# Late edge groups gather normalised source rows from DRAM

## The chip, the cores and the metric

One core of a Trainium2 chip. The metric is the device time of one launch in microseconds, lower is better. Engines are named as in the profile: PE (matmul, with PEld its weight loads), DVE (vector), ACT (scalar, activations), POOL (GpSimd) and SP (sync, which issues plain DMAs).

## The reference

One message-passing layer over N = 50000 nodes and E = 25000 edges, rows of H = 128 float32, edges sorted by target:

```
h        = max(layernorm(x), 0)
em       = relu(layernorm([h[src], h[dst]] @ msg_w + msg_b) * g + beta) * edge_weight
messages = segment_sum(em, dst) / counts          (0 where a node has no edge)
gate     = sigmoid(h @ gate_w + gate_b)
h_new    = relu(layernorm([h, messages] @ upd_w + upd_b) * g + beta)
out      = x + gate * h_new + (1 - gate) * h
```

`layernorm` of x has no gain or shift, so `h` of a node depends on its row of x alone. Both ends of an edge need `h`, not x; the last line needs x of the target.

## The kernel before

**Two stages, in groups of 512 rows.** A group is 128 partitions times G = 4 rows. The node stage runs NG = 98 groups over all nodes as if none had an edge (message zero) and stores the result to `out`. The edge stage runs EG = 49 groups of 512 edges, sums the messages along the sorted edges, computes the update for each edge's target, and scatters the rows of targets with edges over `out` (where an edge is not its target's last, the index is out of bounds and nothing is written). So scatters must come behind the node stores.

**Software pipeline.** Each engine runs the same list of steps; in step s it works on group s, s-1, ... at different stages. Node: x loaded by SP (`node_step`, L505), statistics in DVE step s (L715), `nb` = -mean * rstd (`minus_mean`, L385) and `h` = relu(x * rstd + nb) on ACT in step s+1 (`node_h`, L1093, into `hrow`, 4 buffers), transposed by PE (`flip`, L1200), multiplied, then `mix` (L452: out = x + (1-gate) * h, on DVE in step s+4, into `o`, 4 buffers) and `final` in step s+6. SP stores `o` of group s-8 in step s, and `xload` has XS = 8 buffers. The last six node steps run together with edge steps 0 to 5.

Edge: for group g, source rows and target rows of x have been gathered into a slot of `ring` (RING = 32 slots, each with a source and a target half). DVE step g takes the statistics of both (L917 and L938), with `moment` (L362) in place of an aggregate. ACT step g+1 computes `h` of the source rows into `hrow` (L1145), then of the target rows into `h_dst` (L1151); PE step g+1 flips both (L1276, L1297); then the message product (step g+2), its scaling (`gamma_m`, step g+3), the running sum (step g+4), the update (step g+5), `mix` (step g+7, into `o[g % 4]`) and `final` (step g+8). At the end of the edge stage, from step 49, steps only drain and get shorter.

**POOL** issues all gathers and scatters, one indirect DMA for each 128 rows, in an order written out by hand:

1. The source rows of groups 0 to 4 (EARLY = 5).
2. Beside the node stage, spread over its 98 groups and paced by each group's `mix` (L631 to L644): all other source and target rows of groups 0 to 31, and target rows of groups 35 to 48 (STAGED = 14), which SP stores to DRAM and reloads by plain DMA in the edge stage.
3. Source rows of groups 32 to 38 (AHEAD = 7), as soon as `h` of the group 32 back has been computed (L647).
4. A wait for all node stores, then for each edge group g: wait for `final` of g and for the flips of g+6, four scatters (L667), and a share of the refills (L668): the list is spread over groups 0 to 35 (REFILLED = 36) and holds the source rows of groups 39 to 48 and the target rows of groups 32 to 34.

`mix` of group g waits until the scatter of group g-4 has landed, since both use `o[g % 4]`:

```python
                if fin and not drained:
                    ed["rest"].after(dve, g)
                    if beyond(g, 4):
                        dve.wait_ge(s_scat[g.at % 4], g.rounds(16 * G))
```

Everything behind that on DVE (sums, mix, moments of the newest group) waits with it. In the draining steps (from 49) the same wait stands at the step's start (L906).

**SP** in the edge stage stores the running sums of each group and reloads staged target rows; its last waits are for all stores and scatters.

Of the kernel before, what the change touches and what calls it, by code (L numbers as in the profile page):

```python
# [42 lines left out]
G = 4  # L43
# [4 lines left out]
EG = J // G  # L48
# [6 lines left out]
AHEAD = 7  # L55
# [95 lines left out]
def build(nc, x, src, dst, edge_weight, msg_w, msg_b, msg_g, msg_beta, upd_w, upd_b, upd_g, upd_beta,  # L151
# [3 lines left out]
    with ctx:  # L155
# [12 lines left out]
        staged_dram = nc.dram_tensor("staged_target_rows", (STAGED * P, G * H), f32).ap()  # L168

# [123 lines left out]
        s_st = sem4("node_rows_stored")  # L293
        s_gsrc = sem4("source_rows_gathered")
# [66 lines left out]

        def moment(L, g, n, which):  # L362

            s4 = (g.at + 1) % 4
            v = st[:, g.at % 4, 0:n, :]
            if which == 0:
                nc.vector.tensor_tensor(mv[:, s4, 0:n, 0], v[:, :, 1], v[:, :, 4], ALU.add)
                nc.vector.tensor_tensor(s_dif[:, 0:n], v[:, :, 1], v[:, :, 4], ALU.subtract)
                L.mark(nc.vector.tensor_tensor(s_var[:, 0:n], v[:, :, 2], v[:, :, 5], ALU.add))
            elif which == 1:  # L370
                L.mark(nc.vector.tensor_tensor(s_dif[:, 0:n], s_dif[:, 0:n], s_dif[:, 0:n], ALU.mult))
            else:
                L.mark(nc.vector.scalar_tensor_tensor(mv[:, s4, 0:n, 1], s_dif[:, 0:n], H / 4, s_var[:, 0:n],
                                                      ALU.mult, ALU.add))

        def logs(act, d, s, k, scale=1.0):
            one_mark(d["ln"], act, s, nc.scalar.activation(lnv[:, s.at % 4, 0:k], mv[:, s.at % 4, 0:k, 1], ACT.Ln,  # L377
                                                           bias=eps_col[:, :], scale=scale))

        def rstds(act, d, s, k):  # L380
            act.wait_ge(d["ln"].sem, s.times(1, 1))
            one_mark(d["rstd"], act, s, nc.scalar.activation(rs[:, s.at % 4, 0:k], lnv[:, s.at % 4, 0:k], ACT.Exp,
                                                             scale=-0.5))

        def minus_mean(dve, d, g, n, factor=-1.0):  # L385
            d["rstd"].after(dve, g.back(-1))
            s4 = (g.at + 1) % 4
            one_mark(d["nb"], dve, g, nc.vector.scalar_tensor_tensor(  # L388
                nb[:, s4, 0:n], mv[:, s4, 0:n, 0], factor, rs[:, s4, 0:n], ALU.mult, ALU.mult))
# [96 lines left out]
        def _(sp):  # L486
# [68 lines left out]
            for i in range(4):  # L555
                sp.wait_ge(s_st[i], 16 * len(range(i, NG, 4)))
                sp.wait_ge(s_sums[i], 16 * len(range(i, EG, 4)))
                sp.wait_ge(s_scat[i], 16 * G * len(range(i, EG, 4)))
# [5 lines left out]
        def _(pool):  # L564
# [36 lines left out]
            def gather(dest, rows, idx, s):  # L601
                pool.indirect_dma_start(out=dest, out_offset=None, in_=rows,  # L602
                                        in_offset=bass.IndirectOffsetOnAxis(ap=idx, axis=0),
                                        **(if_tail if rows is x else {})).then_inc(s, 16)
# [19 lines left out]
            for g in range(EARLY):  # L624
                for k in range(G):
# [3 lines left out]
                        for part in ((gather_dst,) if g < EARLY else (gather_src, gather_dst)) for k in range(G)]  # L629
# [28 lines left out]
            for g in range(EG):  # L658
# [10 lines left out]
                for part, q, k in refills[refilled:upto]:  # L669
                    if k == 0 and part is gather_src:  # L670
                        ed["h"].after(pool, Group(q - RING), 1)
                    elif k == 0:
                        ed["mix"].after(pool, Group(q - RING))
                    assert q - RING <= g + (AHEAD if part is gather_src else 0)
                    part(q, k)
# [9 lines left out]
        def _(dve):  # L685
# [203 lines left out]
            def edge_step(s, node=None):  # L889
# [24 lines left out]
                if new:  # L914
                    dve.wait_ge(s_gsrc[s.at % 4], s.rounds(G * 16, G * 16))
                    L = ed["stats"]
                    row_stats(L, s, slot(s, 0), 0)  # L917
                if live(s.back(1), EG):
                    minus_mean(dve, ed, s.back(1), 2 * G, -0.5)
# [133 lines left out]
        def _(act):  # L1053
# [49 lines left out]
            def edge_step(s, node=None):  # L1103
# [6 lines left out]
                logs(act, ed, s, 4 * G, 1.0 / H)  # L1110
                rstds(act, ed, s, 4 * G)
# [29 lines left out]
                if live(g, EG):  # L1141
# [3 lines left out]
                    H_.mark(h_rows(g, hrow[:, (g.at + NG) % 4], slot(g, 0), 0))  # L1145
# [4 lines left out]
                if live(g, EG):  # L1150
                    H_.mark(h_rows(g, h_dst[:, (g.at + NG) % XS], slot(g, 1), G))  # L1151
# [47 lines left out]
        def _(pe):  # L1199
# [53 lines left out]
            def edge_step(s):  # L1253
# [92 lines left out]
```

## Time and profile before

| | |
|---|---|
| median of 3 runs | 909.52 us (909.29 to 910.0) |
| profiled execution: time | 908.32 us |
| profiled execution: span, first to last instruction | 906.6 us |
| mean granted clock of TensorE | 0.924 |
| DMA, whole span | 107.96 MB |

The profiler records one execution. Busy time doesn't count register, branch, semaphore and DMA-issuing instructions of SP; a GpSimd indirect DMA is shown as the time that POOL spends on it, not that of its data. The engine's next instruction can start before the one shown has ended, so two starts are a better measure of what an instruction costs than its duration. "L602" is a line of the kernel; L602 is the helper `gather`, L607 `scatter`, L353 `row_stats`, L395 `h_rows`, L454 `mix_row`, L480 `final`, L388 `minus_mean`, L894 the `omg` instruction at the start of a DVE edge step. `ring<-in_x,src_i` is a gather of source rows, `ring<-in_x,gidx` one of target rows, `work<-in_x,gidx` one of target rows that will be staged, `out<-work,sidx` a scatter.

### The profile page before, as it was taken

Reading aid. Unit: us, or ns where it says so; the run is one execution under the profiler, and the core shown is the slowest. Engines: PE = TensorE matmul, PEld = TensorE weight load, DVE = VectorE, ACT = ScalarE, POOL = GpSimd, SP = SyncE. Lnnn points to the kernel's source line nnn. Section 1 sums busy time; section 2 is a strip of 40 time slices with the busy share of each in tenths; the row PEclk is TensorE's granted clock in tenths of the full one; section 3 lists DMA queues with packets and bytes.
Section 4 is the critical chain, followed back from the end, with each engine's and each line's share of the span. In section 5 each row is a group of like instructions: output and inputs, shape, how many; then the busy total and the mean of one; then the engine's idle time right before and its main releaser. Section 6 shows DMA issues by size and latency. Waiting matters only on the chain.

```text
span 906.6 us, 20426 instructions
## 1 busy us (share of the span) xinstructions
PE 664.2 (73%) x4448; PEld 530.6 (59%) x4448; DVE 847.5 (93%) x3820; ACT 834.8 (92%) x3476; POOL 608.9 (67%) x602
## 2 busy tenths in 40 slices
PE   1877777877777777768578778777787787877871
PEld 0555555655555556555466667666676676666760
DVE  6799999999999999999998999999999999999994
ACT  2799999999999999999789999999999999999972
POOL 4777776666666666666557777657776666664467
PEclk9999999899999999999869998999989999899885
DMA  5355555556556566555223232332211211211111
GB/s 152 97 177 168 175 166 172 162 174 194 177 179 185 182 179 187 176 184 162 73 68 101 66 105 84 103 100 81 83 63 62 70 58 64 71 52 55 58 63 34
DMA packets 60436, 107.96 MB, mean 119 GB/s; under 512 B 14566, under 2 KB 16438, under 8 KB 60370
## 3 DMA queue, kind: packets, MB, share of 16 engines
q1 hardware_dynamic: 39756, 71.88, 23.7%
q0 software_dynamic: 18912, 34.84, 14.4%
q10 hardware_dynamic: 1702, 0.53, 0.3%
q8 instruction: 21, 0.34, 0.2%
q14 instruction: 45, 0.37, 0.1%
HBM read 56.01 MB, written 55.12 MB: 123 GB/s over the span
## 4 chain that ended last, share of the span: by engine, by line
ACT 44%; DVE 36%; issue 10%; PE 4%; POOL 3%; DVEq 1%; ACTq 1%; DMA 1%; POOLq 0%
ACT junk L402 11%; DVE work L752 9%; DVE work L454 9%; ACT hrow L395 9%; ACT xload L395 7%; DVE st L353 6%; ACT work L433 6%; POOL out L607 3%; DVE mv L359 3%; ACT at L1069 2%; ACT work L1126 2%; ACT work L1124 2%; DVE work L731 2%; ACT lnv L377 2%; DVE e L444 2%
## 5 line engine op out<-in xcount | busy, mean ns | idle before, releaser
L607 POOL DMA_INDIRECT out<-work,sidx x196 | 201.7, 1029 | 121.9 <-issue 57.6
L602 POOL DMA_INDIRECT ring<-in_x,src_i x196 | 205.0, 1046 | 79.0 <-issue 54.6
L602 POOL DMA_INDIRECT ring<-in_x,gidx x140 | 142.1, 1015 | 51.0 <-issue 39.0
L395 ACT ACTIVATE hrow<-xload,nb,rs 128x128 f32<-128x128 f32 x392 | 164.4, 530 | 1.6 <-DVE nb L388 1.6
L402 ACT ACTIVATE junk<-py 128x128 bf16<-128x128 f32 x588 | 155.2, 296 | 1.0 <-PE py L1289 1.0
L402 ACT ACTIVATION_READ_ACCUMULATOR junk<-py 128x1 f32 x588 | 133.6, 230 | 0.0
L1203 PE MATMUL pa<-ident,work 128*128 128x128 f32 x376 | 62.6, 290 | 92.6 <-DVE work L731 92.4
L1245 PE MATMUL py<-w_u,work 128*128 128x129 f32 x784 | 119.6, 298 | 0.0
L1245 PEld LDWEIGHTS py<-w_u,work 128*128 128x128 f32 x784 | 99.9, 200 | 21.8 <-issue 21.8
L1203 PE MATMUL pt<-ident,hrow 128*128 128x128 f32 x588 | 101.6, 301 | 13.1 <-ACT hrow L395 12.9
L454 DVE SCALAR_TENSOR_TENSOR work<-hrow,omg,xload 128x128 f32<-128x128 f32 x392 | 108.5, 338 | 0.0
L1203 PEld LDWEIGHTS pa<-ident,work 128*128 128x128 f32 x376 | 40.6, 144 | 115.6 <-issue 112.1
L752 DVE SCALAR_TENSOR_TENSOR work<-pm,gt,work 128x128 f32<-128x128 f32 x376 | 105.1, 341 | 0.0
L1268 PE MATMUL pm<-w_all,work 128*128 128x128 f32 x392 | 98.3, 340 | 0.0
L353 DVE BATCH_NORM_STATS2 st<-xload 128x6 f32<-128x128 f32 x392 | 98.0, 278 | 0.1
L1270 PE MATMUL pm<-w_all,work 128*128 128x128 f32 x392 | 93.6, 329 | 0.0
L1203 PEld LDWEIGHTS pt<-ident,hrow 128*128 128x128 f32 x588 | 76.4, 156 | 21.6 <-ACT hrow L395 20.7
L353 DVE BATCH_NORM_STATS2 st<-ring 128x6 f32<-128x128 f32 x392 | 84.8, 278 | 0.2
L602 POOL DMA_INDIRECT work<-in_x,gidx x56 | 55.6, 994 | 42.3 <-DVE work L454 42.3
L1287 PE MATMUL py<-w_all,at 128*128 128x128 f32 x392 | 82.6, 293 | 0.0
L1268 PEld LDWEIGHTS pm<-w_all,work 128*128 128x128 f32 x392 | 74.8, 237 | 12.7 <-issue 12.7
L395 ACT ACTIVATE hrow<-ring,nb,rs 128x128 f32<-128x128 f32 x196 | 82.3, 532 | 0.0
(170 smaller groups left out, 1832.6 us busy)
## 6 DMA issues: line engine op xcount, KB each, us to landing
xload<-in_x SPq DMA_DIRECT2D x98, 256.0 KB
out<-work SPq DMA_DIRECT2D x98, 256.0 KB
running_sums<-acc SPq DMA_DIRECT2D x49, 256.0 KB, 2.1
staged_target_rows<-work SPq DMA_DIRECT2D x14, 256.0 KB, 3.6
ring<-staged_target_rows SPq DMA_DIRECT2D x14, 256.0 KB, 3.1
ring<-in_x,src_i POOLq DMA_INDIRECT x196, 3.0
out<-work,sidx POOLq DMA_INDIRECT x196, 2.2
ring<-in_x,gidx POOLq DMA_INDIRECT x140
```

What stands on the lines that cost most here:

```text
L353: last = nc.vector.bn_stats(st[:, g.at % 4, at + m, :], rows[:, m, :])
L395: last = nc.scalar.activation(dest[:, m, :], rows[:, m, :], ACT.Relu, bias=nb[:, s4, at + m:at + m + 1], scale=rs[:, s4, at + m:at + m + 1])
L402: last = nc.scalar.activation(junk[:, j, k, :], prod[:, k, 0:H], ACT.Square, scale=scale, accum_out=mv[:, slot, at + k, 1:2])
L454: return nc.vector.scalar_tensor_tensor(dest[:, k, :], h[:, k, :], omg[:, g.at % 4, k:k + 1], xr[:, k, :], ALU.mult, ALU.add)
L602: pool.indirect_dma_start(out=dest, out_offset=None, in_=rows, in_offset=bass.IndirectOffsetOnAxis(ap=idx, axis=0), **(if_tail if rows is ...
L607: pool.indirect_dma_start(out=out, out_offset=bass.IndirectOffsetOnAxis(ap=idx, axis=0), in_=rows, in_offset=None, **if_tail).then_inc(s, 16)
L752: last = nc.vector.scalar_tensor_tensor(o[:, f.at % 4, k, :], pm[:, k, :], gt[:, f.at % 4, k:k + 1], o[:, f.at % 4, k, :], ALU.mult, ALU.add)
L1203: last = nc.tensor.transpose(dest[:, k * H:(k + 1) * H], rows[:, k, :], ident[:, :])
L1245: last = nc.tensor.matmul(py[:, g.at % 2, k, 0:H + 1], ht_dst[:, g.at % 4, k * H:(k + 1) * H], w_u1[:, :], start=False, stop=k % 2 == 1)
L1268: nc.tensor.matmul(pm[:, k, :], ht_src[:, g.at % 2, k * H:(k + 1) * H], w_all[:, 0, :], start=False, stop=False)
L1270: last = nc.tensor.matmul(pm[:, k, :], ht_dst[:, (g.at + NG) % 4, k * H:(k + 1) * H], w_all[:, 1, :], start=False, stop=k == G - 1)
L1287: nc.tensor.matmul(py[:, g.at % 2, k, 0:H], at_[:, g.at % 2, k * H:(k + 1) * H], w_all[:, 3, :], start=False, stop=False)
```

## The change

- The node stage stores `hrow` of every group (256 KB each, 25.7 MB in all) to a new DRAM tensor `normalised_rows`. SP issues the store of group s-4 in step s, behind the store of `out` of group s-8. ACT waits for it before it overwrites the buffer.
- Edge groups from LATE = 16 gather their source rows from there. For these groups DVE takes no statistics of the source half, `moment`, `minus_mean`, the logarithm and the reciprocal root work on a narrower range, ACT computes no `h` of source rows, and PE transposes the gathered rows straight from the ring. The target half is as before; ACT's two marks for `h` now stand behind its first two and last two rows.
- POOL's order: beside the node stage, source rows of groups 5 to 15 alone and target rows of 0 to 31. Then a wait for all stores of normalised rows, the source rows of groups 16 to 27 (UPFRONT = 12) in one go, then scatters and refills as before, the refills now being source rows of groups 28 to 48 and target rows of 32 to 34 over the same 36 groups.
- SP's small bias load moves from behind the first eight node loads to ahead of the load of node group 4.

```diff
-AHEAD = 7
+LATE = 16
+UPFRONT = 12
+        h_dram = nc.dram_tensor("normalised_rows", (N, H), f32).ap()
...
     (SP, node_step)
+                q = s.back(4)
+                if live(q, NG):
+                    nd["h"].after(sp, q)
+                    if q.turn is None and q.at == NG - 1:
+                        sp.wait_ge(s_hst[(q.at - 1) % 4], q.back(1).rounds(16, 16))
+                    sp.dma_start(rows(h_dram, q), hrow[:, q.at % 4]).then_inc(s_hst[q.at % 4], 16)
...
             for g in range(1, XS):
+                if g == 4:
+                    sp.wait_ge(s_bsplit, 1)
+                    sp.dma_start(bias3[:, :], bias_b[0:1, :, :]).then_inc(s_b3, 16)
                 node_step(Group(g))
-            sp.wait_ge(s_bsplit, 1)
-            sp.dma_start(bias3[:, :], bias_b[0:1, :, :]).then_inc(s_b3, 16)
...
     (POOL)
-                gather(slot(Group(g), 0)[:, k, :], x, src_i[:, c:c + 1], s_gsrc[g % 4])
+                gather(slot(Group(g), 0)[:, k, :], h_dram if g >= LATE else x, src_i[:, c:c + 1], s_gsrc[g % 4])
...
-                        for part in ((gather_dst,) if g < EARLY else (gather_src, gather_dst)) for k in range(G)]
+                        for part in ((gather_src, gather_dst) if EARLY <= g < LATE else (gather_dst,)) for k in range(G)]
...
-            for g in range(AHEAD):
-                ed["h"].after(pool, Group(g), 1)
+            for i in range(4):
+                pool.wait_ge(s_hst[i], 16 * len(range(i, NG, 4)))
+            for g in range(LATE, LATE + UPFRONT):
                 for k in range(G):
-                    gather_src(g + RING, k)
-            refills = [(part, g, k) for g in range(RING, EG)
-                       for part in (((gather_src,) if g >= RING + AHEAD else ()) + ((gather_dst,) if g < DIRECT else ()))
+                    gather_src(g, k)
+            refills = [(part, g, k) for g in range(LATE + UPFRONT, EG)
+                       for part in ((gather_src,) + ((gather_dst,) if RING <= g < DIRECT else ()))
                        for k in range(G)]
...
     (DVE, edge_step)
                 if new:
-                    dve.wait_ge(s_gsrc[s.at % 4], s.rounds(G * 16, G * 16))
                     L = ed["stats"]
-                    row_stats(L, s, slot(s, 0), 0)
+                    if not late(s):
+                        dve.wait_ge(s_gsrc[s.at % 4], s.rounds(G * 16, G * 16))
+                        row_stats(L, s, slot(s, 0), 0)
...
     (ACT, node_h)
                     nd["nb"].after(act, g)
+                    if beyond(g, 4):
+                        act.wait_ge(s_hst[g.at % 4], g.rounds(16))
...
     (ACT, edge_step)
-                    H_.mark(h_rows(g, hrow[:, (g.at + NG) % 4], slot(g, 0), 0))
+                    if late(g):
+                        H_.mark(h_rows(g, h_dst[:, (g.at + NG) % XS, 0:2], slot(g, 1)[:, 0:2], G))
+                    else:
+                        if g.at < 4:
+                            act.wait_ge(s_hst[(g.at + NG) % 4], 16 * len(range((g.at + NG) % 4, NG, 4)))
+                        H_.mark(h_rows(g, hrow[:, (g.at + NG) % 4], slot(g, 0), 0))
...
-                    H_.mark(h_rows(g, h_dst[:, (g.at + NG) % XS], slot(g, 1), G))
+                    a = 2 if late(g) else 0
+                    H_.mark(h_rows(g, h_dst[:, (g.at + NG) % XS, a:G], slot(g, 1)[:, a:G], G + a))
...
     (PE, edge_step)
-                    ed["h"].after(pe, g, 1)
-                    one_mark(ed["flip"], pe, g, flip(pt[:, 0, :], hrow[:, (g.at + NG) % 4]))
+                    if late(g):
+                        pe.wait_ge(s_gsrc[g.at % 4], g.rounds(G * 16, G * 16))
+                        one_mark(ed["flip"], pe, g, flip(pt[:, 0, :], slot(g, 0)))
+                    else:
+                        ed["h"].after(pe, g, 1)
+                        one_mark(ed["flip"], pe, g, flip(pt[:, 0, :], hrow[:, (g.at + NG) % 4]))
```

## Rows read from the trace of the kernel before

**Rows 1.** Profile page: its head, and busy time by engine

```profile
span 906.6 us, 20426 instructions
...
PE 664.2 (73%) x4448; PEld 530.6 (59%) x4448; DVE 847.5 (93%) x3820; ACT 834.8 (92%) x3476; POOL 608.9 (67%) x602
```

**Rows 2.** Windows, 300 to 400 us (length, busy by engine, clock, DMA share)

```profile
300.00:400.00 100.00, 73.65 (x511) 55.01 (x512) 96.14 (x489) 96.31 (x397) 69.37 (x70) 0.98 0.61 183
```

**Rows 3.** Timeline of DVE in the edge stage (start us, duration us, instruction)

```profile
503.74 0.35 DVE L454 SCALAR_TENSOR_TENSOR work<-xload,omg,ring 128x128 f32<-128x128 f32 x1
...
505.98 0.27 DVE L894 TENSOR_SCALAR omg<-gt 128x4 f32<-128x4 f32 x1
...
506.84 0.86 DVE L353 BATCH_NORM_STATS2 st<-ring 128x6 f32<-128x128 f32 x4
507.85 0.17 DVE L388 SCALAR_TENSOR_TENSOR nb<-mv,rs 128x8 f32<-128x8 f32 x1
...
510.74 0.87 DVE L353 BATCH_NORM_STATS2 st<-ring 128x6 f32<-128x128 f32 x4
511.52 0.68 DVE L942 SCALAR_TENSOR_TENSOR acc<-acc,cont_wb 128x512 f32<-128x512 f32 x1
...
514.62 0.27 DVE L894 TENSOR_SCALAR omg<-gt 128x4 f32<-128x4 f32 x1
...
832.14 0.35 DVE L454 SCALAR_TENSOR_TENSOR work<-xload,omg,ring 128x128 f32<-128x128 f32 x1
```

**Rows 4.** Timeline of POOL from the end of the node stage

```profile
463.54 1.20 POOL L602 DMA_INDIRECT ring<-in_x,src_i  x1 [3.98 <-DVE work L454]
...
477.80 1.99 POOL L602 DMA_INDIRECT ring<-in_x,src_i  x1 [0.30 <-issue]
...
503.37 1.09 POOL L607 DMA_INDIRECT out<-work,sidx  x1 [0.30 <-issue]
504.76 1.50 POOL L607 DMA_INDIRECT out<-work,sidx  x1 [0.31 <-issue]
506.57 1.21 POOL L607 DMA_INDIRECT out<-work,sidx  x1 [0.30 <-issue]
...
509.37 1.05 POOL L602 DMA_INDIRECT ring<-in_x,gidx  x1 [0.30 <-issue]
```

**Rows 5.** Windows of POOL (columns: length, busy, clock, DMA share, GB/s)

```profile
503.37:550.26 46.89, 37.13 (x33) 0.89 0.26 86
550.26:850.00 299.74, 188.77 (x183) 0.91 0.22 72
881.14:904.80 23.66, 18.48 (x18) 0.59 0.11 36
```

**Rows 6.** Chain of waits, inside one edge step

```profile
605.34 1.52 ACT hrow L395 x4
```

**Rows 7.** Groups of POOL's instructions by line, from 463.5 us

```profile
L602 POOL DMA_INDIRECT ring<-in_x,src_i x68 | 76.3, 1122 | 24.4 <-issue 19.2 <-DVE work L454 4.0 <-ACT xload L395 0.9
L602 POOL DMA_INDIRECT ring<-in_x,gidx x12 | 13.3, 1108 | 3.7 <-issue 3.0 <-PE pt L1203 0.3 <-DVE work L454 0.3
```

**Rows 8.** The same groups, 0 to 463.5 us

```profile
L602 POOL DMA_INDIRECT work<-in_x,gidx x56 | 55.6, 994 | 42.3 <-DVE work L454 42.3
```

**Rows 9.** SP's stores near the stage's end; DMA issues with us to landing

```profile
448.88 17.33 SPq L516 DMA_DIRECT2D out<-work  x3
...
running_sums<-acc SPq DMA_DIRECT2D x49, 256.0 KB, 2.1
...
out<-work,sidx POOLq DMA_INDIRECT x196, 2.2
```

**Rows 10.** Timeline of the drain: DVE's last edge group, POOL's last issue

```profile
891.64 0.69 DVE L480 TENSOR_TENSOR work<-work 128x512 f32<-128x512 f32 x1 [0.43 <-ACT work L433]
...
903.82 0.98 POOL L607 DMA_INDIRECT out<-ring,tidx  x1 [0.30 <-issue]
```

**Rows 11.** DMA queues: packets, MB, share of the 16 engines

```profile
q1 hardware_dynamic: 39756, 71.88, 23.7%
```

More of the change, by code:

```diff
@@ L293, in build @@
         s_st = sem4("node_rows_stored")
+        s_hst = sem4("normalised_rows_stored")
         s_gsrc = sem4("source_rows_gathered")
@@ L360, in aggregate, with late @@
             L.mark(last)
+        def late(g):
+            return g.at >= LATE
         def moment(L, g, n, which):
-            s4 = (g.at + 1) % 4
-            v = st[:, g.at % 4, 0:n, :]
+            s4, a = (g.at + 1) % 4, G if late(g) else 0
+            v = st[:, g.at % 4, a:n, :]
             if which == 0:
-                nc.vector.tensor_tensor(mv[:, s4, 0:n, 0], v[:, :, 1], v[:, :, 4], ALU.add)
-                nc.vector.tensor_tensor(s_dif[:, 0:n], v[:, :, 1], v[:, :, 4], ALU.subtract)
-                L.mark(nc.vector.tensor_tensor(s_var[:, 0:n], v[:, :, 2], v[:, :, 5], ALU.add))
+                nc.vector.tensor_tensor(mv[:, s4, a:n, 0], v[:, :, 1], v[:, :, 4], ALU.add)
+                nc.vector.tensor_tensor(s_dif[:, a:n], v[:, :, 1], v[:, :, 4], ALU.subtract)
+                L.mark(nc.vector.tensor_tensor(s_var[:, a:n], v[:, :, 2], v[:, :, 5], ALU.add))
@@ L370, in moment, with logs @@
             elif which == 1:
-                L.mark(nc.vector.tensor_tensor(s_dif[:, 0:n], s_dif[:, 0:n], s_dif[:, 0:n], ALU.mult))
+                L.mark(nc.vector.tensor_tensor(s_dif[:, a:n], s_dif[:, a:n], s_dif[:, a:n], ALU.mult))
             else:
-                L.mark(nc.vector.scalar_tensor_tensor(mv[:, s4, 0:n, 1], s_dif[:, 0:n], H / 4, s_var[:, 0:n],
+                L.mark(nc.vector.scalar_tensor_tensor(mv[:, s4, a:n, 1], s_dif[:, a:n], H / 4, s_var[:, a:n],
                                                       ALU.mult, ALU.add))
-        def logs(act, d, s, k, scale=1.0):
-            one_mark(d["ln"], act, s, nc.scalar.activation(lnv[:, s.at % 4, 0:k], mv[:, s.at % 4, 0:k, 1], ACT.Ln,
+        def logs(act, d, s, k, scale=1.0, a=0):
+            one_mark(d["ln"], act, s, nc.scalar.activation(lnv[:, s.at % 4, a:k], mv[:, s.at % 4, a:k, 1], ACT.Ln,
@@ L378, in logs, with rstds, minus_mean @@
                                                            bias=eps_col[:, :], scale=scale))
-        def rstds(act, d, s, k):
+        def rstds(act, d, s, k, a=0):
             act.wait_ge(d["ln"].sem, s.times(1, 1))
-            one_mark(d["rstd"], act, s, nc.scalar.activation(rs[:, s.at % 4, 0:k], lnv[:, s.at % 4, 0:k], ACT.Exp,
+            one_mark(d["rstd"], act, s, nc.scalar.activation(rs[:, s.at % 4, a:k], lnv[:, s.at % 4, a:k], ACT.Exp,
                                                              scale=-0.5))
-        def minus_mean(dve, d, g, n, factor=-1.0):
+        def minus_mean(dve, d, g, n, factor=-1.0, a=0):
@@ L388, in minus_mean @@
             one_mark(d["nb"], dve, g, nc.vector.scalar_tensor_tensor(
-                nb[:, s4, 0:n], mv[:, s4, 0:n, 0], factor, rs[:, s4, 0:n], ALU.mult, ALU.mult))
+                nb[:, s4, a:n], mv[:, s4, a:n, 0], factor, rs[:, s4, a:n], ALU.mult, ALU.mult))
         def h_rows(g, dest, rows, at):
@@ L556, in _ @@
                 sp.wait_ge(s_st[i], 16 * len(range(i, NG, 4)))
+                sp.wait_ge(s_hst[i], 16 * len(range(i, NG, 4)))
                 sp.wait_ge(s_sums[i], 16 * len(range(i, EG, 4)))
@@ L603, in gather @@
                                         in_offset=bass.IndirectOffsetOnAxis(ap=idx, axis=0),
-                                        **(if_tail if rows is x else {})).then_inc(s, 16)
+                                        **({} if rows is sums_dram else if_tail)).then_inc(s, 16)
             def scatter(rows, idx, s):
@@ L669, in _ @@
                 for part, q, k in refills[refilled:upto]:
-                    if k == 0 and part is gather_src:
-                        ed["h"].after(pool, Group(q - RING), 1)
-                    elif k == 0:
+                    if k == 0 and q >= RING and part is gather_src:
+                        ed["flip"].after(pool, Group(q - RING), 1)
+                    elif k == 0 and q >= RING:
                         ed["mix"].after(pool, Group(q - RING))
-                    assert q - RING <= g + (AHEAD if part is gather_src else 0)
+                    assert q - RING <= g + (5 if part is gather_src else 0)
                     part(q, k)
@@ L914, in edge_step @@
                 if new:
-                    dve.wait_ge(s_gsrc[s.at % 4], s.rounds(G * 16, G * 16))
                     L = ed["stats"]
-                    row_stats(L, s, slot(s, 0), 0)
+                    if not late(s):
+                        dve.wait_ge(s_gsrc[s.at % 4], s.rounds(G * 16, G * 16))
+                        row_stats(L, s, slot(s, 0), 0)
                 if live(s.back(1), EG):
-                    minus_mean(dve, ed, s.back(1), 2 * G, -0.5)
+                    minus_mean(dve, ed, s.back(1), 2 * G, -0.5, G if late(s.back(1)) else 0)
                 q = s.back(3)
@@ L1109, in edge_step @@
                     ed["square_m"].after(act, s.back(3))
-                logs(act, ed, s, 4 * G, 1.0 / H)
-                rstds(act, ed, s, 4 * G)
+                a = G if late(s.back(1)) else 0
+                logs(act, ed, s, 4 * G, 1.0 / H, a)
+                rstds(act, ed, s, 4 * G, a)
                 if node is not None and live(node.back(4), NG):
```

## The prediction

> **What bounds the kernel now.** I read the page's totals first, then the stretches, then one step of the edge stage engine by engine, and last the GpSimd queue, because the change moves work onto it. The totals [rows 1] show DVE and ACT busy for over nine tenths of the span and POOL for two thirds. That average hides two stages. In the node stage DVE and ACT are both at 96 of 100 us and the 16 DMA engines at 0.61 [rows 2]. In the edge stage the step repeats exactly: the `omg` instruction that opens a step on DVE starts at 505.98 and at 514.62 [rows 3], so a step takes 8.64 us, and DVE and ACT are both full in it. POOL comes third, with four scatters and one or two refill gathers a step.
>
> How full POOL is decides this case. Each indirect DMA holds POOL for about 1 us and the next starts 0.30 us later [rows 4], so unstretched issues come 1.28 to 1.35 us apart (0.98 and 1.05 with the gap, rows 4, 10). Once a step one is stretched to about 1.5 and the next to about 1.2: the one that starts at 504.76 ends at 506.26, over the `omg` of 505.98. From 463.54 to 503.37 POOL issued 28 gathers without a real gap, 1.42 us each; then 33 issues in 46.89 us [rows 5], again 1.42. Only later does it wait for anything: between 550 and 850 it is busy 189 of 300 us with 183 issues, and with 0.30 of gap for each some 56 us are truly idle.
>
> **The change, part by part.** (1) *What groups 16 to 48 save.* On DVE the four statistics of the source rows go, 0.78 us (a block of four starts at 510.74, the instruction behind it at 511.52, rows 3); the moment instructions only narrow. On ACT four `h` activations go, 1.52 us [rows 6]. ACT then has slack and DVE sets the step: 8.64 - 0.78 = 7.86, or 7.63 if the wait of 0.23 ahead of `nb` goes too (from 506.84 to 507.85 is 1.01 where the block needs 0.78). Over 33 groups that is 26 to 33 us, if nothing else holds the step.
>
> (2) *What moves to POOL in the edge stage.* Before, source and target gathers of groups 0 to 31 are issued beside the node stage, and 68 + 12 gathers fall behind 463.5 [rows 7]. After, the sources of groups 16 to 31 must wait for the node rows, so there are 48 gathers up front and 84 + 12 = 96 refills: 144 instead of 80. The 64 moved ones were cheap where they stood, since POOL waited there for the node steps' `mix` [rows 8]; taking them away from there saves nothing, as DVE and ACT are the full ones.
>
> (3) *When the gathers up front start.* POOL leaves the node loop behind the `mix` of node group 97, as before, so at 463.54 [rows 4]. The new wait for the stores of normalised rows costs 0 there: SP issues the last of them at about the time of the node stores that begin at 448.88, and a 256 KB store lands in 2 to 4 us (2.1 for the running sums) [rows 9]. The cover is 10 us; without it, POOL would start later by the landing.
>
> (4) *The sum on POOL.* 28 gathers end at 503.37, as now. Twenty more at 1.42: 531.8. Before, scatter(0), the four row scatters of edge group 0, started at 503.37; now at 531.8. It needs 5.3 us to issue and 2.2 to land [rows 9]: 539. DVE's `mix` of group 4 waits for it, as `o` has four buffers; it would have run at 503.74 (group 1, rows 3) + 3 x 8.64 = 529.7. So DVE stalls 9 us there, and behind it in its queue the moments, the sums and, through them, ACT and PE. From there POOL is the bound: a group costs four scatters and 96/36 = 2.67 gathers, 6.67 x 1.42 = 9.5 us, more than the 8.64 of an early step and the 7.7 to 7.9 of a late one, and every DVE step waits at mix(g+4) for scatter(g). 36 groups and the tail's gather: 241 x 1.42 = 342, to 874. Groups 36 to 48 have 52 scatters, with the tail 54 issues. In the last stretch that is free of waits today 18 issues take 23.66 us [rows 5], 1.31 each, fewer of them stretched; I take 1.33: 72 us, to 946. The end lies 1.8 us behind the last issue (906.6 less 903.82 and 0.98, rows 1, 10): span 947.8.
>
> (5) *Is DVE out of the way at the end?* mix(39) ran at 832.14 [rows 3]; now it waits for scatter(35), landed at about 872.7, 40.6 later. From there to final(48), which ended at 892.3 [rows 10], three late steps save 2.4: 930 to 933. POOL reaches scatter(48) at about 939.5, so it stays the bound, by 7 us.
>
> (6) *The node stage.* Each step stores another 256 KB, and SP gets one more wait and one more DMA a step. The SP queue moved 71.88 MB in 23.7% of the 16 engines' span [rows 11], 334 GB/s. 25.7 MB more are 77 us over some 420: +0.18 on the 0.61, less 0.04 for the 64 gathers, about 0.75. ACT's new wait is for the store of group g-4. That is issued behind `final` of g-8, about three steps of 4.6 us ahead, against 2 to 4 us of landing. The loads of x now also queue behind `h` of five groups back, and are still over two steps ahead. I take 0, between -3 (fewer GpSimd issues beside DVE) and +10. The bias load, moved ahead of the load of node group 4, costs 0: three node steps on DVE cover the later loads.
>
> **Sum.** The profiled execution had 906.6 of span in 908.32, so 947.8 gives 949.5. The median of the runs is 1.2 above that execution, inside my error; I say 949. The disputed size is the stretch of the issues. At no stretch 197 scatters take 1.29 and 146 gathers 1.33: 463.5 + 254 + 194 = 912, a time of 915 to 916, still slower than now. Half the stretch gives 932. I take all of it, because the 61 issues in a row had the same DVE instructions beside them.
>
> The trace shows the stretched issues over the step's `omg` and `final` [rows 3, 4]. SBUF — State Buffer in the Trainium skill (SBUF: two separate sides) says that GpSimd can't write descriptors while DVE runs a two-port fast-mode instruction, and gives a DMA that grows from about 620 to 3100 ns. At that price, an estimate from the page, 48 steps with 1.8 us more than I take would come to about 1035; rows 4 show 0.5 and 0.2 us, and the measurement decides.
>
> **The rivals.** *A, POOL keeps pace (faster):* the saving of (1) stands, 908.3 less 26 to 33: 875 to 882. For it: 56 us truly idle on POOL between 550 and 850. Against: 64 x 1.42 = 91 us are added. It decides at 7.8 / 6.67 = 1.17 us an issue, and rows 4, 10 have none under 1.28. Chance 0.06, with other ways to be faster.
> *B, bound by POOL but little stretched:* the DVE step now follows a landing, and its fast instructions may fall where POOL is between issues: 915 to 932. Chance 0.22.
> *C, the stores are paid in the node stage:* if bursts at a share of 0.75 land over a step late, each per cent of 420 us is 4.2; paid in full they are the 77 us of (6), up to 1026; likelier 955 to 975. Against: over two steps of cover. Chance 0.05. The same page of the Trainium skill (A bandwidth-pool intuition that's wrong) says that HBM is almost always the end-to-end bottleneck; the share in rows 2 doesn't bear it out here.
> *D, a longer lock:* every step stretches an issue as the worst one, 1.99 at 477.80 [rows 4], 1.0 over instead of 0.7: 48 x 0.3 = 14 more, 963. It is the skill's lock taken at the worst row. Chance 0.03.
> *E, no measurable change:* saving and deficit cancel, 906 to 912: needs less than no stretch. Chance 0.02.
> *Forecast:* bound by POOL at about 1.4 us an issue, 932 to 960: 0.62.
>
> **How the numbers follow.** What a measurement of this kernel can tell from no change is about 0.2%, 1.8 us. Slower is 0.62 + 0.22 + 0.05 + 0.03 = 0.92, no change 0.02, faster 0.06. The range 920 to 962 holds the forecast and most of B, and leaves out A, E and nearly all of C and D.
>
> **What would show it.** Right: behind 463.5 POOL without waits to the end, 48 gathers first, the first scatter near 532; a period on DVE of 9.4 to 9.6 us for groups 4 to 39 with idle ahead of L454, put down to scatters; ACT far from full in the edge stage; the node stage ending within 3 us of before. Wrong: POOL waiting for `final` in mid-stage, a late period of 7.7 to 7.9 (A); issues of 1.3 us on average in a row (B); DVE waiting for x, or ACT for stores, in the node stage (C).

## The result, and the profile after

| | before | after |
|---|---|---|
| median | 909.76 us (4 runs: 909.29 to 911.79) | 941.93 us (4 runs: 941.4 to 942.47) |
| ratio | | 1.0349 (95%: 1.0331 to 1.0367) |
| span of the profiled execution | 906.6 | 939.7 |

The changed kernel is 32 us slower, 3.5%. The forecast was 949, with a range of 920 to 962.

The page of the changed kernel: its head, busy time by engine, the shares of the chain that ended last, and SP's DMA queue (they answer to [rows 1, 11]).

```profile
span 939.7 us, 20532 instructions
...
PE 684.6 (73%) x4448; PEld 545.7 (58%) x4448; DVE 817.3 (87%) x3688; ACT 786.2 (84%) x3344; POOL 620.3 (66%) x602
...
q1 hardware_dynamic: 53868, 97.58, 29.4%
...
POOL 35%; DVE 34%; issue 18%; PE 6%; ACT 4%; DVEq 1%; DMA 0%; POOLq 0%; ACTq 0%; SPq 0%
```

DVE and ACT each lost 30 to 49 us of busy time and the span grew by 33. In the chain POOL leads with 35%, where the kernel before had ACT with 44% and POOL with 3%:

```profile
ACT 44%; DVE 36%; issue 10%; PE 4%; POOL 3%; DVEq 1%; ACTq 1%; DMA 1%; POOLq 0%
```

Windows of all engines in the changed kernel (length, busy time of PE, PEld, DVE, ACT, POOL, then clock, DMA share and GB/s; the first answers to [rows 2]).

```profile
300.00:400.00 100.00, 77.25 (x510) 57.64 (x508) 95.89 (x485) 95.20 (x394) 53.73 (x54) 0.95 0.73 232
550.00:850.00 300.00, 231.93 (x1519) 195.39 (x1517) 246.34 (x990) 232.18 (x1044) 234.12 (x217) 0.87 0.25 79
```

The second of these stretches in the kernel before, all engines:

```profile
550.00:850.00 300.00, 237.24 (x1635) 201.85 (x1634) 292.67 (x1182) 294.61 (x1249) 189.03 (x184) 0.91 0.22 72
```

The node stage is as it was (95.9 and 95.2 of 100 us), with the DMA share at 0.73 instead of 0.61. In the edge stage DVE has fallen from 98% to 82% and ACT from 98% to 77%. POOL's 234 us with 217 issues leave 66 us, which is the gap of 0.30 behind each one: POOL never waits.

POOL's groups from 463.5 us on [rows 7], L624 being the scatter and L619 the gather:

```profile
L624 POOL DMA_INDIRECT out<-work,sidx x196 | 210.0, 1071 | 59.8 <-issue 58.6 <-PE pt L1231 0.9 <-DVE work L489 0.3
L619 POOL DMA_INDIRECT ring<-normalised_rows,src_i x132 | 144.7, 1096 | 43.9 <-issue 39.9 <-DVE work L463 4.0
L619 POOL DMA_INDIRECT ring<-in_x,gidx x12 | 12.3, 1029 | 3.7 <-issue 3.7
```

POOL's timeline, around the points of the sum [rows 4]:

```profile
463.62 1.20 POOL L619 DMA_INDIRECT ring<-normalised_rows,src_i  x1 [3.99 <-DVE work L463]
...
504.84 1.52 POOL L619 DMA_INDIRECT ring<-normalised_rows,src_i  x1 [0.30 <-issue]
506.66 1.23 POOL L619 DMA_INDIRECT ring<-normalised_rows,src_i  x1 [0.30 <-issue]
...
530.76 0.99 POOL L619 DMA_INDIRECT ring<-normalised_rows,src_i  x1 [0.30 <-issue]
532.05 1.02 POOL L624 DMA_INDIRECT out<-work,sidx  x1 [0.30 <-issue]
...
864.38 1.14 POOL L619 DMA_INDIRECT ring<-normalised_rows,src_i  x1 [0.30 <-issue]
865.83 1.02 POOL L624 DMA_INDIRECT out<-work,sidx  x1 [0.31 <-issue]
...
936.98 0.98 POOL L624 DMA_INDIRECT out<-ring,tidx  x1 [0.30 <-issue]
```

The 48 gathers start at 463.62 and end with the one at 530.76; the first scatter starts at 532.05. The last refill gather is the one at 864.38; from 865.83 on there are only the last 54 issues. None of the 342 issues behind the first starts more than 0.32 us after the end of the one before it.

One late step on DVE, with the wait that now sets it:

```profile
702.75 0.68 DVE L961 SCALAR_TENSOR_TENSOR acc<-acc,cont_wb 128x512 f32<-128x512 f32 x1
706.88 0.35 DVE L981 SCALAR_TENSOR_TENSOR acc<-acc,cont_wb 128x128 f32<-128x128 f32 x1 [3.45 <-issue]
...
709.40 0.29 DVE L912 TENSOR_SCALAR omg<-gt 128x4 f32<-128x4 f32 x1
709.47 0.68 DVE L489 TENSOR_TENSOR work<-work 128x512 f32<-128x512 f32 x1
710.10 0.16 DVE L397 SCALAR_TENSOR_TENSOR nb<-mv,rs 128x4 f32<-128x4 f32 x1
```

Behind L961 DVE stands still for 3.45 us. The next instruction is L981, the running sum, which in program order comes behind `wait_ge(s_scat...)`; the profile calls it "issue" since no DMA landing is matched to it. Over the whole run these waits add up, and ACT's follow from them (us in total, times, longest):

```profile
ACT lnv L386 <- DVE mv L382: 75.2, 36, 7.8
...
DVE acc L981 <- issue: 67.2, 33, 8.7
```

### The profile page after: what moved, and what is told of

Read it like the earlier page. It is cut to its first block, busy times and chain, and to the rows that moved or that the text cites. A ratio compares the mean times of both kernels' runs of the same rounds, so it can differ in the third digit from the quotient of the medians.

```text
span 939.7 us, 20532 instructions
## 1 busy us (share of the span) xinstructions
PE 684.6 (73%) x4448; PEld 545.7 (58%) x4448; DVE 817.3 (87%) x3688; ACT 786.2 (84%) x3344; POOL 620.3 (66%) x602
## 4 chain that ended last, share of the span: by engine, by line
POOL 35%; DVE 34%; issue 18%; PE 6%; ACT 4%; DVEq 1%; DMA 0%; POOLq 0%; ACTq 0%; SPq 0%
POOL out L624 20%; POOL ring L619 16%; DVE work L770 8%; DVE work L463 8%; DVE st L358 6%; DVE mv L364 3%; DVE work L749 2%; ACT hrow L404 2%; PE py L1273 2%; DVE e L453 2%; ACT junk L411 1%; PE pt L1231 1%; DVEq L114 1%; DVE omg L459 1%; PE pa L1231 1%
## 5 line engine op out<-in xcount | busy, mean ns | idle before, releaser
L624 POOL DMA_INDIRECT out<-work,sidx x196 | 210.0, 1071 | 59.8 <-issue 58.6
L619 POOL DMA_INDIRECT ring<-in_x,gidx x140 | 141.0, 1007 | 79.5 <-DVE work L463 43.5
L619 POOL DMA_INDIRECT ring<-normalised_rows,src_i x132 | 144.7, 1096 | 43.9 <-issue 39.9
L981 DVE SCALAR_TENSOR_TENSOR acc<-acc,cont_wb 128x128 f32<-128x128 f32 x196 | 68.0, 347 | 67.5 <-issue 67.2
L1273 PE MATMUL py<-w_u,work 128*128 128x129 f32 x784 | 121.8, 302 | 0.0
L386 ACT ACTIVATE lnv<-mv,eps_col 128x8 f32<-128x8 f32 (+2 forms) x158 | 50.6, 320 | 82.0 <-DVE mv L382 75.2
L619 POOL DMA_INDIRECT work<-in_x,gidx x56 | 55.7, 995 | 91.0 <-DVE work L463 88.9
L463 DVE SCALAR_TENSOR_TENSOR work<-hrow,omg,xload 128x128 f32<-128x128 f32 x392 | 108.5, 339 | 0.0
L1296 PE MATMUL pm<-w_all,work 128*128 128x128 f32 x392 | 103.2, 355 | 0.0
L1298 PE MATMUL pm<-w_all,work 128*128 128x128 f32 x392 | 98.3, 343 | 0.0
L619 POOL DMA_INDIRECT ring<-in_x,src_i x64 | 64.4, 1006 | 41.8 <-DVE work L463 17.0
L1296 PEld LDWEIGHTS pm<-w_all,work 128*128 128x128 f32 x392 | 79.4, 251 | 14.0 <-issue 14.0
L1231 PE MATMUL pt<-ident,hrow 128*128 128x128 f32 x456 | 79.5, 302 | 8.0 <-ACT hrow L404 7.8
L404 ACT ACTIVATE xload<-ring,nb,rs 128x128 f32<-128x128 f32 x196 | 85.1, 525 | 0.0
```

The source lines that it names most:

```text
L404: last = nc.scalar.activation(dest[:, m, :], rows[:, m, :], ACT.Relu, bias=nb[:, s4, at + m:at + m + 1], scale=rs[:, s4, at + m:at + m + 1])
L463: return nc.vector.scalar_tensor_tensor(dest[:, k, :], h[:, k, :], omg[:, g.at % 4, k:k + 1], xr[:, k, :], ALU.mult, ALU.add)
L624: pool.indirect_dma_start(out=out, out_offset=bass.IndirectOffsetOnAxis(ap=idx, axis=0), in_=rows, in_offset=None, **if_tail).then_inc(s, 16)
L981: S.mark(nc.vector.scalar_tensor_tensor(acc[:, m.at % 4, k, :], before, cont_wb[:, m.at * 2 * G + k:m.at * 2 * G + k + 1], acc[:, m.at % 4 ...
L1231: last = nc.tensor.transpose(dest[:, k * H:(k + 1) * H], rows[:, k, :], ident[:, :])
L1273: last = nc.tensor.matmul(py[:, g.at % 2, k, 0:H + 1], ht_dst[:, g.at % 4, k * H:(k + 1) * H], w_u1[:, :], start=False, stop=k % 2 == 1)
```

## The experiments

All are compared with the kernel before run beside them. In experiments 1 to 6 it took 910 us. Six runs came to two other chips, on which the kernel before took 1022 and 1024 us; they stand in a table of their own at the end of this section.

**1. The order of the DMAs alone.**

```diff
         def late(g):
-            return g.at >= LATE
+            return False
...
-                gather(slot(Group(g), 0)[:, k, :], h_dram if g >= LATE else x, src_i[:, c:c + 1], s_gsrc[g % 4])
+                gather(slot(Group(g), 0)[:, k, :], x, src_i[:, c:c + 1], s_gsrc[g % 4])
```

> The changed kernel's DMAs in its order (stores of normalised rows, 48 gathers up front behind them, 96 refills), but every group computes h of its source rows as before and gathers them from x. Theory 1 (POOL's issues in the edge stage are the bound, the saved work lies beside them): 938 to 946 us, as the changed kernel's 942, a first scatter at 532 and a step of about 9.1 us. Theory 2 (the gathers from the new tensor are slower or later, or the late path's new waits cost the time): clearly under 942, towards 910 to 930. Theory 3 (the saving reached the time in full and something else costs 60): 968 to 975.

Measured: 934.16 us, ratio 1.0262 (1.0229 to 1.0295). POOL's groups from 463.5 us on:

```profile
L624 POOL DMA_INDIRECT out<-work,sidx x196 | 203.4, 1038 | 59.8 <-issue 57.1 <-PE pt L1231 2.4 <-DVE work L489 0.3
L619 POOL DMA_INDIRECT ring<-in_x,src_i x132 | 143.1, 1084 | 43.9 <-issue 39.6 <-DVE work L463 4.0 <-PE pt L1231 0.3
```

That is 4 us under Theory 1's band. With none of the work saved the kernel takes 24 us more than before, with the 33 groups' work saved 32. So the order of the DMAs (the moved gathers, with the stores that experiment 2 prices at nothing) accounts for 24 of the 32 us, and all that the change saves on DVE and ACT buys nothing; it even comes with 8 us more. Those 8 lie in POOL's issues: 1.038 and 1.084 us on average here against 1.071 and 1.096 in the changed kernel. Over 343 issues the mean distance is 1.36 us here ((930.2 + 1.0 - 464.4) / 343) and 1.38 there. Why the issues of the changed kernel are longer no run shows.

**2. The stores alone.** The kernel before with the stores and the new waits of SP and ACT; nothing reads the new tensor. The kernels of this series differ in LATE and UPFRONT alone; source rows of groups below LATE are gathered from x as before, those of groups up to 31 beside the node stage:

```diff
-LATE = 16
-UPFRONT = 12
+LATE = 49
+UPFRONT = 7
...
-            for g in range(LATE, LATE + UPFRONT):
+            for g in range(min(LATE, RING), min(LATE, RING) + UPFRONT):
+                if g >= RING:
+                    ed["h" if g - RING < LATE else "flip"].after(pool, Group(g - RING), 1)
...
-            refills = [(part, g, k) for g in range(LATE + UPFRONT, EG)
-                       for part in ((gather_src,) + ((gather_dst,) if RING <= g < DIRECT else ()))
+            refills = [(part, g, k) for g in range(min(LATE + UPFRONT, RING), EG)
+                       for part in (((gather_src,) if g >= min(LATE, RING) + UPFRONT else ()) +
+                                    ((gather_dst,) if RING <= g < DIRECT else ()))
```

> The kernel before with the stores of normalised rows added (and the bias load moved): same order of gathers as before, nothing reads the new tensor. Theory 1: the stores hide in the node stage, 908 to 913 us, node stage ending within 1 us of before (POOL's gathers behind it start at 463.5). Theory 2 (the stores take part of the loss): 915 to 940.

Measured: 908.56 us, ratio 0.9982 (0.997 to 0.9993). The 25.7 MB of stores cost nothing on this chip. In the median the loads and stores of the changed kernel's node stage land in under a step of 4.6 us (KB each, median us to landing):

```profile
xload<-in_x SPq DMA_DIRECT2D x98, 256.0 KB, 3.7
normalised_rows<-hrow SPq DMA_DIRECT2D x98, 256.0 KB, 3.6
```

**3. LATE = 32, UPFRONT = 7.** POOL's edge stage as before (80 gathers), the saving for groups 32 to 48 alone.

> Only groups 32 to 48 take their source rows from the normalised rows; the sources of groups 16 to 31 are gathered beside the node stage as before, so that the edge stage has 80 gathers as before. Theory 1: no deficit on POOL, and 17 steps on DVE shorter by 0.78 to 1.0 us: 893 to 897 us. Theory 2 (reading the new tensor costs as much as it saves): 908 us or more.

Measured: 889.17 us, ratio 0.9782 (0.9758 to 0.9805), better than either theory's number: 21 us for 17 groups, 1.2 a group. The steps are 7.44 us long. One of them on DVE and the same moment on ACT:

```profile
743.48 0.30 DVE L915 TENSOR_SCALAR omg<-gt 128x4 f32<-128x4 f32 x1
743.55 0.68 DVE L489 TENSOR_TENSOR work<-work 128x512 f32<-128x512 f32 x1
744.17 0.16 DVE L397 SCALAR_TENSOR_TENSOR nb<-mv,rs 128x4 f32<-128x4 f32 x1
744.26 1.12 DVE L474 SCALAR_TENSOR_TENSOR acc<-pm,rs,be_msg 128x128 f32<-128x128 f32 x4
```

```profile
742.89 0.25 ACT L411 ACTIVATION_READ_ACCUMULATOR junk<-pm 128x1 f32 x1
743.59 0.30 ACT L386 ACTIVATE lnv<-mv,eps_col 128x12 f32<-128x12 f32 x1 [0.45 <-DVE mv L382]
```

Before [rows 3], from `omg` at 505.98 to `nb` at 507.85 are 1.87 us; here from 743.48 to 744.17 are 0.69. That is the 1.18 us. Of it 0.78 are the statistics; 0.23 the wait ahead of `nb`; and 0.18 is one that I had not seen: `final` (L489) now starts 0.07 behind `omg` instead of 0.25. What it waits for on ACT, `relu`, ended only at 506.13 before, 0.15 behind the start of `omg`; ACT is no longer late. ACT now waits for DVE (0.45 us ahead of L386) instead of the reverse.

**4. Half the scatters.** Rows 2 and 3 of each group are not scattered, so half of the updated rows are missing from the output.

```diff
-                for k in range(G):
+                for k in range(2):
                     c = g * G + k
                     scatter(o[:, g % 4, k, :], sidx[:, c:c + 1], s_scat[g % 4])
```

(and the counts of the waits for `s_scat` to match)

> The changed kernel with two of each group's four row scatters left out (half of the updated rows are not written). A group of the refill phase costs POOL 4.67 issues, 6.4 us, less than a DVE step. Theory 1: DVE becomes the bound from about group 10, late steps of 7.6 to 7.9 us, 878 to 892 us, of which some 7 us are the stall behind the 48 gathers up front. Theory 2 (POOL's issues are not the bound): over 915 us.

Measured: 867.77 us, ratio 0.9548 (0.952 to 0.9576); 10 us below the expected band; the late step is 7.44 instead of 7.6 to 7.9, and 33 steps of 0.2 to 0.4 less are 7 to 13 us. All engines, 600 to 750 us, and two `omg` in a row on DVE:

```profile
600.00:750.00 150.00, 120.59 (x952) 103.68 (x950) 149.32 (x606) 140.64 (x646) 115.47 (x101) 1.00 0.27 83
```

```profile
685.41 0.16 DVE L912 TENSOR_SCALAR omg<-gt 128x4 f32<-128x4 f32 x1
...
692.84 0.17 DVE L912 TENSOR_SCALAR omg<-gt 128x4 f32<-128x4 f32 x1
```

DVE is at 149.3 of 150 us and the period is 7.43. So with 98 issues fewer the time falls 74 us, and the bound goes back to DVE. This and experiment 1 are the direct evidence for POOL: the first takes the saving away and loses nothing, the second takes 98 issues away and ends below the kernel before.

**5. LATE = 24, UPFRONT = 11.** 112 gathers in the edge stage.

> late24 once more, since in the runs beside its first ones the kernel before itself took 1022 us. Groups 24 to 48 take normalised source rows; 112 gathers in the edge stage. Theory 1 (POOL's issues decide): a refill group costs POOL 5.89 issues at 1.37, 8.1 us; room while steps last 8.64, then behind by 0.6 us a step against late steps of 7.44, which the output buffers take up: 877 to 886 us. Theory 2 (POOL bound already): over 890.

Measured: 900.96 us, ratio 0.9893 (0.9859 to 0.9928): 12 us more than LATE = 32, and over Theory 1's band. POOL, 550 to 750 us, and its last issue:

```profile
550.00:750.00 200.00, 156.75 (x142) 0.93 0.27 84
```

```profile
895.72 0.98 POOL L624 DMA_INDIRECT out<-ring,tidx  x1 [0.30 <-issue]
```

142 issues in 200 us, 1.41 each and no waits: it is bound by POOL already. DVE's own period says the same once its saving has begun and the slack is gone: from 702.69 to 834.77 us 16 steps take 8.26 each, where 5.89 issues of 1.41 are 8.3 and DVE alone needs 7.44. My expectation took the four output buffers as slack and forgot that the 44 gathers up front had used it up. The plain count would have told: at the changed kernel's 1.38 us, 463.6 + 311 issues x 1.38 + 1.8 = 895 for a measured span of 898.

**6. What stretches an issue: `omg`?**

```diff
-                    one_mark(ed["rest"], dve, g, nc.vector.tensor_scalar(omg[:, g.at % 4, :], gt[:, g.at % 4, :], -1.0, 1.0,
-                                                                         ALU.mult, ALU.add))
+                    one_mark(ed["rest"], dve, g, nc.vector.scalar_tensor_tensor(
+                        omg[:, g.at % 4, :], gt[:, g.at % 4, :], -1.0, one4[:, :], ALU.mult, ALU.add))
```

> The changed kernel with the omg instruction as a two-input scalar_tensor_tensor, once more. Theory 1 (omg stretches the issue in flight): the issues of 1.52 and 1.23 us among the 48 gathers up front go, the mean issue of the bound phase falls from 1.37 to about 1.33, 928 to 938 us. Theory 2 (another cause): 940 to 944 and the same stretched issues.

Measured: 941.47 us, ratio 1.0327 (1.0288 to 1.0365), as the changed kernel. POOL, then DVE, in the same microseconds:

```profile
504.39 1.51 POOL L620 DMA_INDIRECT ring<-normalised_rows,src_i  x1 [0.30 <-issue]
506.21 1.24 POOL L620 DMA_INDIRECT ring<-normalised_rows,src_i  x1 [0.30 <-issue]
507.76 1.00 POOL L620 DMA_INDIRECT ring<-normalised_rows,src_i  x1 [0.30 <-issue]
```

```profile
505.64 0.15 DVE L914 SCALAR_TENSOR_TENSOR omg<-gt,one 128x4 f32<-128x4 f32 x1
505.89 0.69 DVE L490 TENSOR_TENSOR work<-work 128x512 f32<-128x512 f32 x1
```

`omg` itself fell from 0.25 to 0.15 us, and the issues over it are stretched as before, 1.51 and 1.24: Theory 2. The traces show in which direction the two touch. In the changed kernel 32 of 39 `omg` between 495 and 860 us last 0.24 to 0.30 us, and each of these ends within 0.04 us of the end of the issue that it lies in, 13 times one of no more than 1.02 us; the other 7 last 0.16 or 0.17. One of the 13, the issue and the `omg` in it:

```profile
697.67 0.99 POOL L619 DMA_INDIRECT ring<-normalised_rows,src_i  x1 [0.30 <-issue]
698.38 0.25 DVE L912 TENSOR_SCALAR omg<-gt 128x4 f32<-128x4 f32 x1
```

In this run all 39 last 0.15 or 0.16. So `omg` in its first form was held by the issue and didn't hold it. What does stretch it was not found. One candidate stays untested: each of the four issues of 1.52 us among the 48 gathers up front lies over the second half of DVE's block of alternating sums and mixes (L981 and L463), which every run of these kernels has.

**7. Two chips on which the kernel before takes 1022 and 1024 us.** `late32_plain`, `late24`, `late24_plain` and `plain_omg` ran on one of them, `late28` and `fused_final` on the other. Edits: LATE = 24 as in 5; `late32_plain` and `late24_plain` are LATE = 32 and 24 with the edit of 6; `plain_omg` is 6; `late28` is LATE = 28, UPFRONT = 8; `fused_final` is the changed kernel with the two 128x512 additions of a step rewritten:

```diff
-            one_mark(d["final"], eng, g, vec.tensor_tensor(dest, dest, t_buf[:, g.at % 4, 0:n, :], ALU.add))
+            one_mark(d["final"], eng, g, vec.scalar_tensor_tensor(
+                dest, dest, 1.0, t_buf[:, g.at % 4, 0:n, :], ALU.mult, ALU.add))
```

(and the same in `beta`)

> The changed kernel with the omg instruction at the start of a DVE edge step written as a two-input scalar_tensor_tensor instead of tensor_scalar, same result. Theory 1 (that instruction stretches the GpSimd issue in flight, by 0.5 and 0.2 us in the 48 gathers, by 0.1 to 0.3 in the bound phase): the 1.52 and 1.23 us issues of the first 48 gathers go, the mean issue of the bound phase falls from 1.37 to about 1.33, 928 to 938 us. Theory 2 (the stretch has another cause, such as the long two-input instructions that follow it): 940 to 944, the same stretched issues.

> Groups 24 to 48 take normalised source rows, 44 gathers up front, refills of 17 groups' targets and sources left: 112 gathers in the edge stage. A refill group costs POOL 5.89 issues, about 8.0 us. Theory 1: POOL has room for it while steps last 8.64 us and falls behind by 0.6 us a step from group 24, which the four output buffers take up: 25 steps shorter by 1.2, 877 to 886 us. Theory 2 (POOL bound already): over 890.

> late32 with the omg instruction as a two-input form. DVE bounds the step there, POOL has room. Theory 1: the step loses only what omg itself was held, under 0.1 us a step: 884 to 890, the 1.5 us issues gone. Theory 2 (the stretched issues hold the step): under 880.

> late24 with the two-input omg. If late24 is partly bound by POOL, 3 to 8 us under late24; if it isn't, within 3 us of it: 874 to 884 us.

> Groups 28 to 48 take normalised source rows, 32 gathers up front and 64 in the refills: 96 in the edge stage, 16 more than before. Theory 1 (the time is the larger of two: DVE's 8.64 us a step up to group 27 and 7.44 behind, 4.8 us under late32's 889; or POOL's count, 463.5 + 294 issues at 1.38 to 1.41 + 1.8 = 871 to 880): 882 to 887 us, and the best of the series 49, 32, 28, 24, 16. Theory 2 (each moved gather costs some time even below the balance): 889 us or more.

> The changed kernel with the two 128x512 additions of a DVE edge step (beta and final) written as scalar_tensor_tensor with a factor of 1, same result. Theory 1 (the two-input tensor_tensor additions stretch the GpSimd issue beside them): mean issue of the bound phase from 1.38 down to about 1.32, and 343 issues carry that to 920 to 930 us. Theory 2 (the stretch comes from elsewhere): 938 to 945 us with the mean issue unchanged.

| kernel | gathers in the edge stage | us | ratio to before on the same chip | ratio in experiments 3, 5 and 6 |
|---|---|---|---|---|
| late32_plain | 80 | 1016.0 | 0.9975 (0.9932 to 1.0018) | 0.9782 (late32) |
| late28 | 96 | 1040.11 | 1.0172 (1.0111 to 1.0233) | not measured |
| late24 | 112 | 1065.98 | 1.0435 (1.0359 to 1.051) | 0.9893 |
| late24_plain | 112 | 1063.34 | 1.042 (1.036 to 1.0479) | not measured |
| plain_omg | 144 | 1070.6 | 1.0507 (1.0436 to 1.0579) | 1.0327 |
| fused_final | 144 | 1067.71 | 1.0426 (1.0364 to 1.0488) | not measured |

None of the expected times can be read on these. From 80 to 112 gathers the ratio grows, as in the other runs; at 112 and 144 the intervals overlap. The three ratios that can be compared are worse here, by 2 to 5.5%, and LATE = 28 could not show whether it beats 32. What these chips lack was not found; no trace of the kernel before was taken there. But `plain_omg` and `plain_omg_again` are one kernel, and their traces show that the time is lost in both stages and that POOL is not the bound here: the 48 gathers up front start at 513.7 instead of 463.2, and behind the first scatter POOL waits 77 us in 43 waits, where it waits for nothing in `plain_omg_again`. So these times say nothing for or against the count of issues. One thing can be read, since the stage change leaves DVE idle for over 30 us while POOL issues its gathers. All engines of `plain_omg`:

```profile
544.00:578.00 34.00, 8.63 (x34) 6.86 (x34) 0.00 (x0) 5.52 (x21) 25.99 (x26) 0.50 0.19 50
600.00:700.00 100.00, 68.78 (x438) 58.33 (x436) 78.86 (x314) 79.28 (x335) 64.24 (x64) 0.85 0.27 83
```

From 544 to 578 us DVE ran nothing, ACT 21 instructions, and POOL made 26 issues in 34 us, 1.30 apart, each shown with 1.00 us. So with DVE idle, and PE and ACT mostly so, no issue is stretched here, where 13 of the first 48 of the changed kernel last over 1.1 us: the stretch comes with work beside it on other engines. Which work, stays open. POOL's groups in `fused_final` and then in `plain_omg`, 620 to 920 us, each on one of the two chips:

```profile
L626 POOL DMA_INDIRECT out<-work,sidx x116 | 120.0, 1035 | 79.8 <-remote 42.9 <-issue 29.4 <-PE pt L1233 7.5
L621 POOL DMA_INDIRECT ring<-normalised_rows,src_i x64 | 65.6, 1024 | 19.5 <-issue 19.5
```

```profile
L625 POOL DMA_INDIRECT out<-work,sidx x114 | 117.8, 1033 | 77.8 <-remote 42.8 <-issue 29.5 <-PE pt L1233 5.5
L620 POOL DMA_INDIRECT ring<-normalised_rows,src_i x65 | 66.6, 1024 | 19.8 <-issue 19.8
```

The means differ by 2 ns at most, which speaks against the two additions as well, but issues are hardly stretched there in either and the chips are not the same, so it is weak evidence.

## Why the prediction was right

The mechanism was the one forecast, and its terms can be held against the run one by one.

- **Start of the gathers (3):** 463.54 forecast, 463.62 measured. The wait for the stores cost nothing.
- **The first scatter (4):** 531.8 forecast, 532.05 measured. The stall at `mix` of group 4: 9 us forecast; the step from the `omg` of group 4 to that of group 5 took 17.46 instead of 8.64, 8.8 more.
- **The bound phase (4):** 241 issues at 1.42 would be 342 us; they took 333.8 (532.05 to 865.83), 1.385 each. This is the whole error of the sum: 947.8 forecast for the span, 939.7 measured. DVE's period follows: 9.3 us on average from 540.82 to 875.64, in steps of 7.4 to 11.1, where 9.4 to 9.6 was named as the sign. The mean of 1.42 came from stretches in which the DVE steps ran at 8.64 us. In the bound phase the issues are stretched less: of the 241 issues 59 last 1.12 to 1.35 us and 3 over 1.45, where of the 33 before [rows 5] it was 5 and 5. It went part of the way to rival B, whose reason was that a DVE step now follows a landing and meets the queue elsewhere; that this is the reason fits the trace but is not shown, since what stretches an issue was not found.
- **The last 54 issues (4):** 72 us forecast, 72.4 measured (865.83 to 936.98 + 0.98 + 0.30).
- **DVE out of the way at the end (5):** right; POOL issues without a wait to the end.
- **The wait on DVE (4):** right, but the idle time stands ahead of L981 and is called "issue", where the sign named was idle ahead of `mix` put down to scatters. The sum and the mix stand behind the same wait.
- **The node stage (6):** 0 forecast; `stores_alone` measured 1.5 us less than before (-0.3 to -0.07%). The DMA share of 0.73 is near the 0.75 worked out. Rival C is out on this chip. On the slower ones nothing excludes it.
- **The saving (1)** was mis-sized: 0.78 to 1.01 us a step by the text, 1.19 measured (8.63 to 7.44). The missing 0.18 is `final` waiting for ACT. It didn't matter for the forecast, as the saving is hidden; for rival A it does. A would have given 908 - 39 = 869. `half_scatters` reached 868, which is near by luck in part, as it still has a stall of 5 us behind the gathers up front (a step of 13.60).
- **The cause of the stretch** was wrong in part: rows 3 and 4 show the stretched issue over `omg`, and I read that as `omg` holding POOL. Experiment 6 shows the reverse. The size held all the same, since it was taken from the rows and not from the cause. It is luck in part: the same count gives 949 for `order_alone` too, which has the same DMAs in the same order and took 934. The exclusive lock of SBUF — State Buffer in the Trainium skill (SBUF: two separate sides), which the one that starts first keeps for its whole instruction, would fit an `omg` that is held until the issue in flight ends. The traces agree in part: an `omg` that starts 0.71 us or more into an issue, and 0.25 or more ahead of its end, is held to its end, but the two that start 0.17 and 0.20 us into theirs in the changed kernel (821.62 and 671.67) last 0.17 like those beside no issue. What holds the issue itself no run here shows.
- **Rival D** is out in the bound phase: the longest of the 241 issues lasted 1.55 us.

What would have been better is in the experiments too: the same idea with LATE = 32 needs no gather moved behind the node stage and gives 889 us, 2.2% under the kernel before and 5.5% under the changed one (0.9782 / 1.0349).

## What to carry to other kernels

Before work is moved between stages, count the instructions of every queue in the stage that receives them: here 343 issues, at the 1.42 and 1.33 us read from the kernel before, gave the end of the kernel within 1%, while DVE and ACT, at 93 and 92% in the totals, had nothing more to say. Where a change saves work on the full engines by giving another queue more, there is a setting at which the two meet (at 80 gathers POOL still waits here, at 112 it does not; 96 was measured on a slower chip only), and the saving is to be had only up to it. A queue that is never first in the totals still has its own stage in which it is nearly full; its truly idle time there (56 us between 550 and 850) is the budget of the change, and 64 issues of 1.4 us are 90.

## What the runs showed of the hardware

- Instructions that run together on two engines prove no cause: the `omg` instruction (TENSOR_SCALAR, 128x4) lasted 0.24 to 0.30 us where a GpSimd issue ended over it, ending with it to 0.04 us, and 0.15 once written as SCALAR_TENSOR_TENSOR; the issue was 1.5 us long in both.
- A GpSimd indirect DMA of 128 rows of 512 bytes takes 1.00 us with 0.30 to the next when DVE is idle and PE and ACT mostly so (`plain_omg`, 544 to 578 us), and 1.36 to 1.42 from one to the next with them busy and nothing to wait for.
- The granted clock of TensorE in the edge stage differed with the step: 0.91 before (550 to 850 us), 0.87 in the changed kernel, where PE waits for stalled steps, and 1.00, the upper level throughout, in `half_scatters` with steps of 7.44 us (600 to 750 us). PE was busy for 79, 77 and 80% of these stretches, so the clock was highest where the steps were shortest and PE had no more idle time than elsewhere.
- The same kernel before took 910 us in experiments 1 to 6 and 1022 and 1024 us on two other chips, and the ratios of three edits differed by 2 to 5.5% between them.
